# FFN matmuls inside the gate stage, weight loads by output block, SiLU in the last stage

## What is computed

```python
xn = layernorm(x)                                    # (2048 tokens, 2048) per core
q, k, v = split(silu(xn @ w_qkv.T))                  # 16 heads of 128
o = lightning_attention(q, k, v)                     # scan over blocks of 256 tokens
o = norm_w * o * rsqrt(mean(o * o) + 1e-6)
gate = sigmoid(xn @ w_gate.T)
s = (gate * o) @ w_out.T
soft = sigmoid(pweight) - sigmoid(nweight)           # (out, in, 4 bit planes)
W = einsum('oin,n->oi', soft, exps * sigmoid(mask)) * scale
g = silu(xn @ W.T + bias)
x = x + s * g
```

## Time and profile before

| | us |
|---|---|
| median of 2 runs | 2416.97 (2416.53 to 2417.41) |
| the profiled execution, its own time | 2414.47 |
| its span on the slowest core (core 4) | 2412.6 |
| spans of the 8 cores | 2392.5 to 2412.6 |
| busy: TensorE, DVE, ACT, POOL | 1633.3, 868.0, 569.0, 191.9 |

### The profile page before, as it was taken

The page is one execution under the profiler, slowest core; times in us unless marked ns, Lnnn a source line. Parts: engine busy times, 40 slices in busy tenths (PEclk is TensorE's granted clock), DMA queues, the critical chain, the costliest instruction groups (busy, mean ns, idle before and its releaser), DMA issues.

```text
span 2412.6 us, 22642 instructions; the slowest of 8 cores (2392.5 to 2412.6 us)
## 1 busy us (share of the span) xinstructions
PE 1633.3 (68%) x7928; PEld 765.3 (32%) x7928; DVE 868.0 (36%) x1613; ACT 569.0 (24%) x827; POOL 191.9 (8%) x308
## 2 busy tenths in 40 slices
PE   1111534554459999388888888888888888277896
PEld 1110211222124444144344434343433434133342
DVE  5555254444550000223333332333333333624445
ACT  2225455555562212311111111111111111100000
POOL 1002322222210000000000000000000000110000
PEclk9999767777779999699999999999999999588998
DMA  9218999999971112012222201222222200498554
GB/s 209 103 55 105 137 154 159 161 161 162 163 135 40 38 40 63 14 27 45 44 44 44 40 22 27 44 44 45 44 44 44 44 18 9 136 192 174 166 170 148
DMA packets 170512, 211.74 MB, mean 88 GB/s; under 512 B 74016, under 2 KB 114976, under 8 KB 166304
## 3 DMA queue, kind: packets, MB, share of 16 engines
q0 software_dynamic: 135936, 109.07, 33.7%
q1 hardware_dynamic: 34464, 101.23, 12.7%
HBM read 277.37 MB, written 41.94 MB: 132 GB/s over the span
## 4 chain that ended last, share of the span: by engine, by line
PE 49%; DMA 26%; DVE 12%; issue 7%; ACT 5%; SPq 1%; POOL 1%; DVEq 0%; ACTq 0%; POOLq 0%
PE pfA L580 29%; DMA pnbg<-nwT 11%; DMA xT_fc<-xT 5%; DMA pnbg<-pwT 5%; PE pfA L453 5%; PE pS L453 5%; ACT sq_b L725 2%; DVE sT_b L676 2%; PE pfA L355 2%; PE pT L612 2%; DMA wout_sb<-woutT 2%; PE pS L355 1%; DVE mneg_c L198 1%; DVE s L905 1%; PE pS L728 1%
## 5 line engine op out<-in xcount | busy, mean ns | idle before, releaser
L580 PE MATMUL pfA<-xnT,wq_sb 128*128 128x512 bf16 x3072 | 724.3, 391 | 44.4 <-ACT q_dim L596 41.4
L580 PEld LDWEIGHTS pfA<-xnT,wq_sb 128*128 128x128 bf16 x3072 | 299.7, 101 | 404.6 <-issue 86.3
L355 PE MATMUL pfA<-xnT,wg_sb 128*128 128x512 bf16 x512 | 143.9, 451 | 301.3 <-ACT gate_stA L365 245.7
L676 DVE TENSOR_TENSOR sT_b<-pS,decT_all 128x512 bf16<-128x512 f32 x128 | 88.4, 691 | 319.0 <-PE pS L664 319.0
L407 DVE TENSOR_TENSOR sgp<-sgp,sgn 128x1024 bf16<-128x1024 bf16 x128 | 88.6, 692 | 261.7 <-ACT sgn L403 261.2
L355 PEld LDWEIGHTS pfA<-xnT,wg_sb 128*128 128x128 bf16 x512 | 56.5, 112 | 388.3 <-issue 349.1
L733 DVE SCALAR_TENSOR_TENSOR O_st<-pO,csb,gate_h 128x256 bf16<-128x256 f32 x128 | 61.9, 484 | 308.0 <-ACT sq_b L725 306.4
L398 ACT ACTIVATE sgp<-pnbg 128x1024 bf16<-128x1024 bf16 x128 | 135.2, 1056 | 141.9 <-DMA pnbg<-pwT 132.2
L897 PE MATMUL pfA<-O_sb,wout_sb 128*128 128x512 bf16 x512 | 125.5, 403 | 48.5 <-DVE s L905 40.5
L403 ACT ACTIVATE sgn<-pnbg 128x1024 bf16<-128x1024 bf16 x128 | 135.1, 1055 | 73.5 <-DMA pnbg<-nwT 66.4
L246 PE MATMUL pT<-id_bf,xntok 128*128 128x128 bf16 x256 | 29.8, 308 | 146.5 <-DVE xntok L235 146.5
(11 more groups left out here) (106 smaller groups left out, 1476.6 us busy)
## 6 DMA issues: line engine op xcount, KB each, us to landing
pnbg<-pwT POOLq DMA_DIRECT2D x128, 256.0 KB, 22.9
pnbg<-nwT POOLq DMA_DIRECT2D x128, 256.0 KB, 23.5
wq_sb<-wqkvT POOLq DMA_DIRECT2D x16, 1536.0 KB, 14.0
xtile<-x SPq DMA_DIRECT2D x16, 1024.0 KB, 5.7
xT_fc<-xT SPq DMA_DIRECT2D x16, 1024.0 KB, 8.3
outT<-outb SPq DMA_DIRECT2D x64, 256.0 KB, 3.5
wg_sb<-wgateT POOLq DMA_DIRECT2D x16, 512.0 KB, 20.6
gate_scr<-gate_stA SPq DMA_DIRECT2D x16, 512.0 KB, 9.2
```

The costliest lines, as they stand in the source:

```text
L355: r = e.matmul(pbank[:], wg_sb[b][:, fc * HD:(fc + 1) * HD], xnT[:, fc * T + tg * 512: fc * T + tg * 512 + 512], start=(fc == 0), stop=(fc ...
L580: r = e.matmul(pfA[par][:], wq_sb[hb][:, fc * 384 + sel * 128: fc * 384 + (sel + 1) * 128], xnT[:, fc * T + tg * 512: fc * T + tg * 512 + ...
L676: tst = sch.op("V", (lambda h, jp: lambda e: e.tensor_tensor(out=sT_b[:, jp * 512:(jp + 1) * 512], in0=pS[jp][:], in1=decT_all[:, h * 512: ...
```

## The change

W is now made by output blocks. `emit_pn_chunk(ic)` becomes `emit_pn_ob(ob)`: for each of 4 bit planes one DMA brings 128 output columns of all 2048 input rows of `pwT`, laid out as 16 blocks of 128 columns per partition (2048 rows of 512 B), into one of two `pnbg` buffers over POOL, cast to bf16. The same piece of `nwT` comes over SP, uncast, into one of two float32 buffers `pnq`. The sigmoids, the subtraction and the multiply-add work on 2048 columns instead of 1024, half as often. With block fc of `WffnT` complete, that block's FFN matmuls can run, so the FFN stage is dissolved: `emit_ffn_ob(step)` stands at the end of each step of the gate stage's loop. It shares the four PSUM banks with the gate groups in the order gate(h), ffn(h), gate(h + 1), each group waiting for the eviction of its bank (`tok_evac`). The FFN banks are evicted by DVE (adding the bias), not by ACT. SiLU is taken in the last stage, by ACT, in place on each `g_fc` after its load. Head 0's `wq_sb` is an ordinary buffer, loaded at the start of the attention stage.

```diff
-    tok_wq0 = sch.op("G", lambda e: e.dma_start(
-        out=wq_sb0[:].rearrange("p (c j) -> p c j", j=384), ...
-    NPSL = 6
-    pnbg = [... f"pnbg{i}", [128, D // 2], BF16 ... for i in range(2 * NPSL)]
+    pnbg = [... f"pnbg{i}", [128, D], BF16 ... for i in range(2)]
+    pnq = [... f"pnq{i}", [128, D], F32 ... for i in range(2)]
...
         for tg in range(NTG):                
-                gi4 = h * NTG + tg
-                pbank = (pfA + pS)[gi4 % 4]
+                cidx = h * 8 + tg
+                pbank = (pfA + pS)[cidx % 4]
...
                     waits=[tok_wg[h], tok_xn,
-                           tok_gst.get(gi4 - 4)], inc=True)
+                           tok_evac.get(cidx - 4)], inc=True)
...
+                tok_evac[cidx] = tok_gst[h * NTG + tg]
...
+        def emit_pn_ob(ob):
+            prev_cast = tok_wob.get(ob - 1)
+            for n in range(NBITS):
+                u = ob * NBITS + n
+                sl = u % 2
+                sp = u % 2
+                tok_pn[(u, 0)] = sch.op("G",
+                    (lambda ob, n, sl: lambda e: e.dma_start(
+                        out=pnbg[sl][:].rearrange("p (c o) -> p c o", o=128),
+                        in_=pwT_ap[n][:, ob * 128:(ob + 1) * 128].rearrange(
+                            "(c p) o -> p c o", p=128)))(ob, n, sl),
+                    waits=[tok_sig.get((u - 2, 0))],
+                    inc=True, sem=f"pn{sl}")
+                tok_pn[(u, 1)] = sch.op("Q", ...
+                    waits=[tok_sig.get((u - 2, 1))],
+                    inc=True, sem=f"pq{sl}")
+                ...
+            tok_wob[ob] = sch.op("V", (lambda ob: lambda e: e.tensor_copy(
+                out=WffnT[:, ob * D:(ob + 1) * D], in_=Wacc[:]))(ob), ...
+
+        def emit_ffn_ob(fc):
+            for tg in range(NTG):
+                cidx = fc * 8 + 4 + tg
+                gidx = fc * NTG + tg
+                pbank = (pfA + pS)[cidx % 4]
+                ...
+                tmm_ = sch.op("T", mmfn(fc, tg, pbank),
+                    waits=[tok_wob[fc], tok_xn, tok_evac.get(cidx - 4)], inc=True)
+                bse = gidx % 2
+                tok_gse[gidx] = sch.op("V",
+                    (lambda fc, tg, pbank, bse: lambda e: e.tensor_scalar(
+                        out=g_st[bse][:], in0=pbank[:],
+                        scalar1=biasW[:, fc:fc + 1], scalar2=1.0,
+                        op0=ALU.add, op1=ALU.mult))(fc, tg, pbank, bse),
+                    waits=[tmm_, tok_gev.get(gidx - 2)],
+                    hard=[tbias], inc=True)
+                tok_evac[cidx] = tok_gse[gidx]
+                tok_gev[gidx] = sch.op("Q", ...
+
+        emit_pn_ob(0)
+        emit_pn_ob(1)
         emit_wg_load(0)
         emit_wg_load(1)
         for step in range(NH):
             emit_gate_head(step)
             if step + 2 < NH:
                 emit_wg_load(step + 2)
             if step + 2 < NFC:
-                emit_pn_chunk(step + 2)
+                emit_pn_ob(step + 2)
+            emit_ffn_ob(step)
...
+        tok_wq[0] = sch.op("G", lambda e: e.dma_start(
+            out=wq_sb[0][:].rearrange("p (c j) -> p c j", j=384), ...
+            waits=tok_ffn_done + [tok_gsd[NH - 1]], inc=True, sem="wq0")
...
+            tok_gl[fc] = sch.op("S", (lambda fc, fb: lambda e: e.activation(
+                out=g_fc[fb][:], in_=g_fc[fb][:], func=AF.Silu))(fc, fb),
+                waits=[tok_gl[fc]], inc=True)
```

More of the change, by code:

```diff
@@ L331, in build_program @@
         tok_gst = {}
+        tok_evac = {}
         tok_pn = {}
@@ L334, in build_program @@
         tok_comb = {}
-        tok_wchunk = {}
+        tok_wob = {}
+        tok_gev = {}
+        tok_gse = {}
         def emit_wg_load(h):
@@ L371, in emit_gate_head @@
                 waits=[tok_gst[h * NTG + NTG - 1]], inc=True, sem="gsd0")
-        HD2 = D // 2
-        def emit_pn_chunk(ic):
-            prev_cast = tok_wchunk.get(ic - 1)
+        def emit_pn_ob(ob):
+            prev_cast = tok_wob.get(ob - 1)
             for n in range(NBITS):
[L378 to L424, removed]
-            tok_wchunk[ic] = sch.op("V", (lambda ic: lambda e: e.tensor_copy(
-                out=WffnT[:, ic * D:(ic + 1) * D], in_=Wacc[:]))(ic),
-                waits=[tok_xn],
-                hard=[tok_comb[(ic * 8 + 7, 1)]], inc=True)
@@ L430, in build_program @@
-        emit_pn_chunk(0)
-        emit_pn_chunk(1)
+                u = ob * NBITS + n
[8 more added lines that the diff above has]
+                    inc=True, sem=f"pn{sl}")
@@ new lines, in emit_pn_ob, with mmfn, f @@
+            tok_wob[ob] = sch.op("V", (lambda ob: lambda e: e.tensor_copy(
+                out=WffnT[:, ob * D:(ob + 1) * D], in_=Wacc[:]))(ob),
+                waits=[tok_xn],
+                hard=[tok_comb[(ob * NBITS + NBITS - 1, 1)]], inc=True)
+        def emit_ffn_ob(fc):
[3 more added lines that the diff above has]
+                pbank = (pfA + pS)[cidx % 4]
+                def mmfn(fc, tg, pbank):
+                    def f(e):
+                        for ic in range(NFC):
+                            r = e.matmul(pbank[:],
+                                     WffnT[:, fc * D + ic * 128: fc * D + ic * 128 + 128],
+                                     xnT[:, ic * T + tg * 512: ic * T + tg * 512 + 512],
+                                     start=(ic == 0), stop=(ic == NFC - 1))
+                        return r
+                    return f
+                tmm_ = sch.op("T", mmfn(fc, tg, pbank),
[9 more added lines that the diff above has]
+                tok_evac[cidx] = tok_gse[gidx]
+                tok_gev[gidx] = sch.op("Q",
+                    (lambda fc, tg, bse: lambda e: e.dma_start(
+                        out=g_dram[fc, :, tg * 512:(tg + 1) * 512], in_=g_st[bse][:]))(fc, tg, bse),
+                    waits=[tok_gse[gidx]], inc=True, sem=f"gev{bse}")
@@ L487, in sbC @@
             return esC.enter_context(nc.sbuf_tensor(name, list(shape), dtype))
-        wq_sb = [wq_sb0, sbC("wq_sb1", (128, NFC * 384), BF16)]
+        wq_sb = [sbC(f"wq_sb{i}", (128, NFC * 384), BF16) for i in range(2)]
         gate_h = [sbC(f"gate_h{i}", (128, T), BF16) for i in range(2)]
```

79 lines of the change are left out of this document (40 added, 39 removed).

## The result

| | before | after |
|---|---|---|
| median, us | 2422.59 (10 runs) | **2788.7** (11 runs, 2777.15 to 2795.61) |
| ratio to before, 95% interval | | 1.1518 (1.1491 to 1.1546) |
| span of the profiled execution, slowest core | 2412.6 | 2783.0 |
| first qkv matmul, us | 956.9 | 1339.8 |

The changed kernel is 15.2% slower: 366 us, where 253 were forecast. Some executions of most kernels take a few per cent longer; the medians here are of all executions, while the ratios and their intervals leave those out.

A forecast was written before the change was run, and what follows sets the result against it. Loads were taken to bound the gate stage. Ring start at 255.5, fourteen 65.0 us steps, 41.5 of last matmuls and 3.0 tail end at 1210 against 956.9: +253, 2670 us. Forecast 2620 to 2730 (0.62), range 2550 to 2785.

The forecast's parts named there:

- The ring: Gate stage: a block's loads, arithmetic and gate matmuls run in turn before the next loads; step 65.0 us against 48.7.
- Tail and gate of a period: After a step's last load: two sigmoids 4.0, subtraction 1.3, multiply-add 2.5, cast 1.2, eviction 0.7, handovers 0.4; then gate 15.9 us.
- The load term: Ring step's loads: 1152 small rows per engine at 30 ns, 34.6 us, plus issue, gate write and slot wait; landed at 39.0.
- Overlap as drawn: Rival: FFN evictions don't hold up the next loads, so only DMA work counts; -154 us, 2263 us; chance 0.03.
- little changed: Rival: lockstep costs about what the FFN's 221 us give back, a step of 44 to 50 us; 2417; chance 0.02.
- Two queues overlap better: Rival: small rows on both queues cost 24 ns, step 59.2 us; +162, 2579 us; faster rows had chance 0.15.
- The nw rows are slow: Rival: SP's small rows aren't pipelined, 44 ns each, step 72.2 us; +365, 2782 us; slower rows had chance 0.15.
- What was costed at nothing: Late wq(0) load in the attention stage (about 14 us if uncovered) and last-stage Silus (35 us without the gap): nothing.
- slow-rows rival: The rival "The nw rows are slow": SP's small rows at 44 ns, 2782 us; chance 0.15.

The follow-up runs named there:

- experiment 1: The changed kernel with one call moved: a block's FFN matmuls and evictions stand ahead of the next block's loads and arithmetic; 2517.25 us, ratio 1.0381.
- experiment 2: The changed kernel with loads issued once their slot is free, each unit followed by one gate group and one FFN group; 2435.06 us, ratio 1.0048.
- (6): The kernel of experiment 2 with both halves on q0 as bf16 and gate outputs written by quarters, still two slots; 2420.04 us, ratio 0.9915.
- (5): The changed kernel with the nw loads on POOL's q0 too, cast to bf16 like pw; 2651.42 us, ratio 1.0943.

## Why the prediction was right, and where it was wrong

- **The ring** is shown. TensorE's gate matmuls are released by DVE's FFN evictions and POOL's wg issue by the gate matmuls, 14 times each, as foretold; moving one line (experiment 1) takes 271 us off and opening it altogether (experiment 2) 354. From 618 to 642 us, while ACT, DVE and the gate matmuls finish, the DMA share is 0.07, the pause of some 25 us that was foretold.
- **Tail and gate of a period.** From the last sigmoid's start (615.9) to the first gate matmul (625.56) 9.6 us, forecast 10.1; the gate 16.6, forecast 15.9. The sizes behind them: sigmoid 1905 ns (forecast 2.0 us), subtraction 1225 ns (1.3), multiply-add 2351 ns (2.5).
- **The load term is the step that failed.** "Both queues use the same 16 engines, [...] so I add them, 256 x 30 = 7.68 us." From the end of the gate to the last load it came to 45.7 us (570.2 to 615.9), forecast 39.0: 6.7 of the 6.9 us by which a period is too long. 6.9 us in 14 periods are 97 us; the same term at the start, six units in 64 to 67 us instead of 46.1, gave 18.5 more (ring from 274, forecast 255.5). Together some 115 us; the forecast was 113 short.
- **Why the term was too small.** The 30 ns came from stretches of 12 and 5 us with one queue at work, on one core. Sustained, with all cores loading, a row cost 39.0 ns (experiment 2) or 38.0 (6), and 22.5 with an idle neighbour (5). 30 lies between and is neither. What the neighbour does was no part of the reasoning at all. Inside a period the miss lies at its beginning: 1.5 us were put in for issue and first byte, and ACT's first sigmoid came 23.8 us after the gate's end, not 18.5. That is 5.3 of the 6.7 us; from there to the last load it is 21.9 us, forecast 20.5. The queues in that period (packets, MB, share), first 573 to 577, then 579 to 586, then 586 to 596:

```profile
q1 hardware_dynamic: 1004, 0.55, 69.5%
...
q0 software_dynamic: 2169, 0.55, 77.9%
q1 hardware_dynamic: 1910, 0.97, 63.0%
...
q0 software_dynamic: 3687, 0.93, 97.5%
q1 hardware_dynamic: 730, 0.37, 18.0%
```

  Issued at 570.5, q0 brings almost nothing until 577, while q1 works alone at 64 ns a row (4 x 16 / 1004); together they reach 27.5 ns (7 x 16 / 4079); then q0, nearly alone, 36 ns. How much of the 5.3 us is q0's late start and how much the neighbour, which loads meanwhile, no run separates.
- **The rivals.** "Overlap as drawn" and "little changed" asked for loads in 21 to 24 us; they took 45.7. "Two queues overlap better" had 24 ns, and the two together do reach 27.5 for a while, but not over the load phase. The Trainium skill (DMA: Bandwidth & Descriptors, Why small descriptors are slow) gave an estimate of 22 ns, and the trace agrees only where the neighbour is idle (22.5 ns). "The nw rows are slow" gave a period of 72.2 us and 2782: its size is right to 0.3 us, but by luck, for its reason fails. With all rows on q0 the first periods are 71.7 and 75.0 us just the same, and q1's rows are slow only beside a loading neighbour. Here is q1 alone on core 3 from 561 to 565, while core 2 loads nothing:

```profile
q1 hardware_dynamic: 1832, 1.03, 99.4%
```

  4 x 16 us / 1832 are 34.9 ns a row, where core 2's q1 had 64 while core 3 loaded.
- **What was costed at nothing** was nothing. The attention stage is 1131 us against 1128 with `wq_sb` loaded late; the first qkv matmul waits 18.8 us for it, while ACT builds its tables. In the last stage the multiply now waits for the Silu and the add no longer for `xT_fc` (first line: waits from 2455 to 2783; second: that tile's share of line 916):

```profile
DVE s L912 <- ACT g_fc L882: 116.7, 15, 14.1
...
  DMA xT_fc<-xT: 8.0, 10
```

  94.9 and 33.9 before: 128.8 then, 124.7 now. The Silu (1910 ns) went into the gap, as the prediction had it.
- **The range** ended at the price of the slow-rows rival. Both sides of the unknown cost were read from rows, but the upper one from one short stretch of one queue; a few us beyond it would have held the time, by luck and not by a better reason.

## What to carry to other kernels

When work is laid under transfers, follow each engine's queue around once: if the instruction that frees a buffer or bank stands behind work that needs the very loads that it lets start, the stage becomes a ring, and every period pays for loads, arithmetic and matmuls one after the other (354 us here, most of it undone by moving one line). Price a transfer by a stretch in which it runs as long, and beside as busy a neighbour core, as it will in the new kernel; a short stretch of one core's trace gives neither bound. And if a new order of work needs narrower rows, widen the unit (two blocks by half the depth) before giving up the order: 2389 to 2279 us here, and 2249 with the gate matmuls moved from behind the last load to beside the loads.

## What the runs showed of the hardware

- The cores work in pairs (0 and 1, 2 and 3, 4 and 5, 6 and 7) on something shared that small rows exhaust: 178 to 182 GB/s written by one core with its neighbour idle, 111 and 96 when both load (364 GB/s read alone, 414 for both together). The Trainium skill (HBM Reference, Specifications) says that the two cores of a pair share about 716 GB/s of their memory; here rows of 512 B reach little over half of that for the pair, so by that figure it is not the plain bandwidth that gives out. What else it is, no run here shows.
- Two cores with a load phase and a compute phase each can slide into opposite phase and gain from it: 71.7 us a period at the start, 54.6 at the end, with nothing changed in the program.
- A row's place counts beside its length: 512-B rows 8 KB apart cost 39.6 ns (38.0 with two slots), side by side 35.5.
- Wider rows pay off up to 1024 B (2389 to 2279 us). With 2048 B the loads still end a little earlier (last cast at 722.9 against 747.5), but the kernel is not faster (2261 against 2249), since two more FFN blocks stand behind them.
- Beside a second queue the first starts later: with the nw rows on q1, q0's first rows of a period came 5.9 to 7.0 us after the wg issue, on all eight cores (issues 5 to 12; 4.8 to 6.6 us with long rows), and 2.5 to 3.4 us with every load on q0. What delays them, no run here shows.
- The price of a row on q1 too hangs on the neighbour: 64 ns while it loads, 34.9 while it doesn't.
